# Attention loop of a two-layer hybrid model: side work at half ticks, the product in two halves, the finish bank kept a tick longer

## What is computed

```python
B, S, E = (2, 512, 256)      # as written; b, s come from x: 4, 1024
H, DC, DR = (16, 64, 128)
HD = E // H                  # 16
...
q = _gelu(jnp.concatenate([q_c, q_r], axis=-1)).reshape(b, s, H, HD).transpose(0, 2, 1, 3)
k = _gelu(jnp.concatenate([k_c, k_r], axis=-1)).reshape(b, s, H, HD).transpose(0, 2, 1, 3)
scores = jnp.einsum('bhqd,bhkd->bhqk', q, k) * scale
causal = jnp.triu(jnp.ones((s, s), dtype=bool), k=1)
scores = jnp.where(causal[None, None], -jnp.inf, scores)
attn = jax.nn.softmax(scores, axis=-1)
out = jnp.einsum('bhqk,bhkd->bhqd', attn, v)
out = out.transpose(0, 2, 1, 3).reshape(b, s, E)
return out @ wo + bo
```

## Time and profile before

| | us |
|---|---|
| median of 3 runs | 5038.63 |
| lowest and highest run | 5031.27, 5047.35 |
| span of the profiled execution | 5046.6 |
| attention loop in it (first `scores_T` to last `finish`) | about 3976 to 4642 |
| TensorE busy in the whole span | 3946.2 (78%) |

### The profile page before, as it was taken

How to read it: one execution, slowest core, us unless ns; L and a number is a source line. 1 busy time by engine, 2 the same in 40 slices (tenths; PEclk the granted TensorE clock), 3 DMA queues, 4 the chain that set the end, 5 groups by cost and what they waited for, 6 DMA issues and landing times.

```text
span 5046.6 us, 49393 instructions
## 1 busy us (share of the span) xinstructions
PE 3946.2 (78%) x15216; PEld 2274.4 (45%) x15218; DVE 2845.7 (56%) x4948; ACT 2217.0 (44%) x4098; POOL 2475.4 (49%) x2152
## 2 busy tenths in 40 slices
PE   6888888759947778897788769977965788887892
PEld 2333333347724445675333346645642333333671
DVE  6999999941146664211888842236334666554422
ACT  5566666321147664112555533333334444445241
POOL 5999999822212333111888944433455311112256
PEclk9999999959968888998888879987986799999896
DMA  5666665422210100321555521123347222211145
GB/s 152 158 161 151 161 160 159 127 77 85 84 56 17 34 26 9 105 102 53 150 153 145 145 82 46 44 90 94 92 131 154 72 40 39 39 27 46 46 137 131
DMA packets 312121, 476.73 MB, mean 94 GB/s; under 512 B 34890, under 2 KB 167990, under 8 KB 311786
## 3 DMA queue, kind: packets, MB, share of 16 engines
q1 hardware_dynamic: 277152, 388.87, 29.1%
q0 software_dynamic: 29184, 76.12, 5.4%
q10 hardware_dynamic: 5504, 8.39, 0.6%
HBM read 375.26 MB, written 97.49 MB: 94 GB/s over the span
## 4 chain that ended last, share of the span: by engine, by line
PE 39%; POOL 7%; DVE 6%; issue 5%; ACT 4%; DMA 3%; SPq 0%; DVEq 0%; ACTq 0%; POOLq 0%; another core or an unknown queue 0%
PE s_gate_up L2305 8%; PE s_result_sum L2321 4%; PE s_out_sum L3676 3%; PE s_hidden_sum L1745 3%; PE s_result_sum L1756 3%; PE s_scores_T L3660 3%; POOL s_h L435 2%; PE s_shared L2961 2%; DVE s_maxima L3308 2%; PE s_scores L3617 2%; POOL s_gathered L1047 1%; PE s_shared L2971 1%; POOL s_h L444 1%; PE s_transposed L2295 1%; PE s_mid_transposed L2314 1%
## 5 line engine op out<-in xcount | busy, mean ns | idle before, releaser
L435 POOL TENSOR_TENSOR s_h<-s_dtu,s_bc 128x1024 f32<-128x1024 f32 x384 | 904.0, 2363 | 78.4 <-PE s_y_sum L477 61.9
L477 PE MATMUL s_y_sum<-s_h,identity 128*128 128x512 f32 x1536 | 776.3, 643 | 158.2 <-POOL s_h L444 150.4
L402 ACT ACTIVATE s_decay<-s_dt,s_A 128x512 f32<-128x512 f32 x768 | 498.3, 681 | 330.2 <-DVE s_h L377 323.4
L477 PEld LDWEIGHTS s_y_sum<-s_h,identity 128*128 128x128 f32 x1536 | 296.5, 203 | 600.4 <-issue 305.3
L3482 ACT ACTIVATE s_weights_T<-s_scores_T 128x1024 f32<-128x1024 f32 (+3 forms) x384 | 292.2, 809 | 311.9 <-PE s_scores_T L3660 309.7
L2305 PE MATMUL s_gate_up<-s_w_gate_up,s_rowsT 128*128 x1184 | 420.5, 488 | 2.8 <-issue 2.4
L3308 DVE TENSOR_REDUCE s_maxima<-s_scores 128x1 f32<-128x512 f32 (+3 forms) x440 | 282.6, 659 | 218.7 <-PE s_scores L3621 140.0
L444 POOL TENSOR_TENSOR s_h<-s_h,s_bc 128x512 f32<-128x512 f32 x288 | 367.1, 1275 | 23.6 <-DVE s_h L370 14.9
L3530 POOL TENSOR_SCALAR_AFFINE_SELECT s_weights_T<-s_weights_T 128x256 f32<-128x256 f32 x256 | 103.2, 408 | 541.2 <-ACT s_weights_T L3482 538.6
L2364 DVE TENSOR_TENSOR s_mid<-s_act,s_gate_up 128x128 f32<-128x128 f32 (+1 forms) x228 | 92.9, 407 | 454.7 <-ACT s_act L2337 430.2
L370 DVE TENSOR_TENSOR_SCAN s_decay<-s_decay,s_carry,s_h 128x512 f32<-128x512 f32 x240 | 303.1, 1276 | 24.5 <-POOL s_clip_flag L2633 13.8
(11 more groups left out here) (533 smaller groups left out, 7739.6 us busy)
## 6 DMA issues: line engine op xcount, KB each, us to landing
s_bc<-s_bc_rows SPq DMA_DIRECT2D x384, 512.0 KB
sorted_results<-s_result SPq DMA_DIRECT2D x160, 128.0 KB
s_w_inter<-in_L_ffn_experts_inter SPq DMA_DIRECT2D x16, 1024.0 KB
s_w_exp_out<-in_L_ffn_experts_out SPq DMA_DIRECT2D x16, 1024.0 KB
s_queries<-parts_of_q SPq DMA_DIRECT2D x96, 128.0 KB
s_keys<-parts_of_k SPq DMA_DIRECT2D x96, 128.0 KB
results_by_token<-zeros SPq DMA_DIRECT2D x16, 512.0 KB, 6.1
s_pair<-results_by_token SPq DMA_DIRECT2D x16, 512.0 KB
```

What stands on the lines that cost most here:

```text
L402: S.e.activation(self.decay[:, (2 * g + d) % 4, :], dt[q // self.passes % 2][:, at, :], ACT.Exp, scale=A[:, at, g % ns:g % ns + 1]).then_i ...
L435: G.e.tensor_tensor(self.h[r][:], dtu[q // self.passes % 2][:, at:at + 2, :], mid(self.bc[r][:, 0, :], 2), ALU.mult).then_inc(*self.fed.up())
L477: made = T.e.matmul(self.y[:, d, :], ident[:], self.h[r][:, d, :], start=False, stop=g % ns == ns - 1)
```

## The change

```diff
@@ Banks.place
-                    if until[b] <= fill and not (b == 0 and any(fill < f + 2 and read >= f for f in fixed))]
+                    if until[b] <= fill and not (b == 0 and any(fill < f + 3 and read >= f for f in fixed))]
@@ attention_stage
-    at_tick = [FIRST + NS * a + NS * i // PER for a in range(2) for i in range(PER)]
+    at_tick = [FIRST + NS * a + 2 * NS * i // PER / 2 for a in range(2) for i in range(PER)]
@@ vector, main
                 beside(2 * s)
+                beside(2 * s + 0.5)
                 if ends(NS * u + s - 4):
                     finish(NS * u + s - 4)
                 beside(2 * s + 1)
+                beside(2 * s + 1.5)
@@ tensor
-        def product(n):
+        def product(n, half):
...
-            T.wait_ge(*weighed.at(2 * n + 1))
+            T.wait_ge(*weighed.at(2 * n + half))
             if diagonal(s):
-                T.wait_ge(*masked.at(2 * (diagonals[-1] * u + diagonals[s]) - 1))
-            if kt == 0:
+                T.wait_ge(*masked.at(2 * (diagonals[-1] * u + diagonals[s]) - 2 + half))
+            if kt == 0 and half == 0:
                 T.wait_ge(*free[7])
-            for j in range(NG):
+            for j in range(2 * half, 2 * half + 2):
                 made = T.e.matmul(ob[32 * j:32 * j + 32, o:CH], V1[u % 2][:, kt, hg * NG + j, :], PT[n % 3][:, j, o:CH],
                                   start=kt == 0, stop=kt == last_kt)
+            if half == 0:
+                return
             made.then_inc(*out_part.up())
@@ tensor, main
                     scores(n, 0)
+                beside(2 * s)
+                if n < N_STEPS:
                     scores(n, 1)
-                beside(2 * s)
+                beside(2 * s + 0.5)
                 if ends(n - 3):
                     finish(group(n - 3))
+                if 0 <= n - 2 < N_STEPS:
+                    product(n - 2, 0)
                 beside(2 * s + 1)
                 if 0 <= n - 2 < N_STEPS:
-                    product(n - 2)
+                    product(n - 2, 1)
+                beside(2 * s + 1.5)
```

## The result

The change made the kernel slower: 5071.9 us (median of 4 runs, 5067.8 to 5075.8) against 5042.6 us for the kernel before beside it (4 runs, 5031.3 to 5047.4). The ratio is 1.0062, with a 95% interval of 1.0046 to 1.0078. The forecast was 5060 us on a base of 5038.6, so +21 where +29 was measured.

A forecast was written before the change was run, and what follows sets the result against it. TensorE was taken to set the loop's pace. Split products +124 us, waits and stalls -83, clock -18 made +23; 2 off for the last unit gave 5038.6 + 21 = 5060 us, range 5015 to 5095.

The forecast's parts named there:

- The price: TensorE in the loop: products whose halves are separated by side work stream twice, in 148 of 192 steps, adding 124 us.
- The bound of 13 us: Lower bound on the added TensorE time: if a half product took half the time, only entry and some exit add.
- the rival in which the halves keep their concurrency: Second half starts while the batch streams, so the change only moves batches: -88 us, 4951 us; chance 0.03.
- The relief by waits: TensorE's PSUM bank waits in the loop: 72 of 105 us go, plus 11 for vanished stalls, together 83 us.
- the division's 41 us: TensorE's waits for bank `misc` after a finish, 41.3 us: the later refill was to remove all 41.
- the waits for the projection: TensorE's waits for ScalarE's and VectorE's parts of the projection, 7.5 + 5.3 + 4.9 us: 5 were to stay.
- The clock: TensorE's time at half clock after stalls, 24 us in eight units: three quarters, 18 us, were to come back.
- The 2 us of the last unit: Last unit, where ScalarE's exponentials set the pace: the few split products are partly covered, so 2 us come off.
- The faster one: Rival: bank waits vanish altogether and the clock stays up, 124 - 148 = -24 us, 5015 us; chance 0.15.
- The slower one: Rival: `misc` waits go, but batches lean on two banks; other waits and clock stay: +78 us, 5117 us; chance 0.10.
- The one with a lower clock: Rival: each unit spends twice the time at 0.50 clock, losing another 24 us: +65 us, 5104 us; chance 0.07.
- the one in which price and relief cancel within 15 us: Rival: kept waits some 20 us and the full clock relief, 5045 us; chance 0.30.

The follow-up runs named there:

- both bank edits: Finish bank kept three ticks, not two, on the kernel before: 5017.3 us; bank of turned maxima held one tick longer on the whole-product-early kernel: 4986.8 us.

## Why the prediction was right

**The price** (124 us): right, by mechanism and size. It is 119 us, in one comparison with the order of batches held fixed. Its parts were read rightly too: 0.99 us for two matmuls of 512 columns, 0.56 and 0.35 us at 256 and 128. The bound of 13 us, and the rival in which the halves keep their concurrency, are out. The entry was counted in full, while part of it lies under the record before it; that may be the 5 us, which I did not measure apart. The estimate from the Trainium skill (draining between tiling modes, "TensorEngine Tiling (Array Packing)", Key Properties, priced from the latency of a single matmul) would have made 139 us; the 119 us speak for the prices from the rows.

**The relief by waits** (83 us): too high, and this is the term that put the forecast under the measured time. Idle time fell by 54 us in place of 72. Line by line: the division's 41 us went, as said. The finish kept 5.5 us and not 12. But the waits for the projection, 17.7 us before, kept 14.3 (4.7 + 3.7 + 2.3 + 1.9 + 1.7) and not 5; the split maxima did not sink from 10.1 to 7, they rose to 15.3 (12.0 + 3.3); the values rose from 3.5 to 6.3; and the reductions kept 7.7 and not 3. The largest of these misses, 9 us, is the projection's, and its reason was that "the bank comes round later". That a later round ends the wait did not hold. The pace does count somewhat, since the split maxima wait 19.8 us with the product whole and early and 15.3 here. But the waits change more with the table: it hands out the banks anew, so that another piece follows in a bank before its reader is done. I did not follow the pieces through the table one by one, so this part is argued. The restarts, at the prediction's 0.16 us a stall, are 7 us for 46 fewer waits, beside the 11 taken.

**The clock** (18 us): near. Time at 0.50 in the loop went from 48 to 7 us, and half of the difference is 20 us. The Trainium skill's rule for the rival ("TensorE: Matmul & The Clock Gate", A second HAM failure mode: many small idle gaps bring the clock down again and again) pointed the right way, but the time at 0.50 does not follow the idle time alone: with 62 or 63 us of idle it was 0, 3 and 27 us.

**The 2 us of the last unit**: they hold. Eight separated products stand there, 6.1 us by the prices of the prediction, and the unit is 4.1 us longer than with the product whole and early.

The sum by what was measured: 119 - 54 - 7 - 20 = +38, and the loops give +37. In these terms the forecast was some 16 us low; that the medians came within 8 us of it is in part luck. They give +29 (+23 to +39 by the interval); the start of the loop moves by up to 22 us between profiled executions whose code ahead of it is the same (by 13 us between two of the changed kernel), so the profiles cannot say more about the rest of the program.

**What was to be seen:** These signs were set on a wider cut of the loop, 672 us before, with its edges. Cut so, the loop of after is 709 us and not some 690, TensorE is busy 647 us and not 670, and it idles 61.5 us, just over the 60 that were named as the sign of a wrong relief. That the narrow cut also shows 690 us is chance. The 670 added the price to the busy time and forgot that the clock and the restarts come off the same number. I also expected the finish's wait to be the largest; it is third.

**The rivals.** The faster one needed under 6 us of kept waits; 51 us of idle stayed. The slower one, waits that only change places, is not what the change did, but both bank edits show its mechanism in small: 19 of 48 us came back in the one, all 20 in the other. The one with a lower clock is out, since the time at 0.50 fell. So is the one in which price and relief cancel within 15 us: the interval begins at +23. ScalarE's and GpSimd's slack held: their busy times are within 5 us of before.

## What to carry to other kernels

Matmuls that share the array by column groups ran as one stream here; count what stands between them before you slot anything in, because a cut by group repeats the whole stream, while a cut along the streamed columns costs only its ends. When an edit bundles a better order with something that adds time, the idle time falls for both reasons, so test the order alone: here it is worth 73 us (0.985), and the kernel with the product whole and early beats both. And a table that keeps a buffer back can move waits as well as remove them; read who comes next in each buffer.

## What the runs showed of the hardware

Splitting a packed product has a fixed price beside the streamed columns: 0.09 us to get from ordinary matmuls into the group and 0.14 us beyond the columns to its end (0.57 us for 256 columns in float32, where the step from 256 to 512 columns takes 0.43). In sum it came out a little lower: 134 cuts along the columns cost 28 us, 0.21 each and not 0.23. And equal idle time does not mean an equal clock: two loops with 62 and 63 us of idle time stood 3 and 27 us at 1.2 GHz. The one with more had its waits gathered, 28.3 us in 23 waits of up to 1.7 us ahead of the finish, and every stretch at the lower clock inside its loop began at the end of one of the longest. Whether their length or their place brought the clock down was not tried; length alone does not settle it, since five of the 13 waits of 1.7 us left the clock up.
